# Decoder layer with two experts per row: the outer stage of the mixture folded into its tiles, left-out rounds moved ahead

## The reference

```python
probs = softmax(flat @ gate_W); topk_w, topk_idx = top_k(probs, 2)
topk_w = topk_w / topk_w.sum(-1)
combine = (one_hot(topk_idx, 8) * topk_w[..., None]).sum(1)
out = 0.5 * gelu(flat @ shared_W + shared_b)
for e in range(8):
    h = gelu(flat @ W1[e] + b1[e])                  # 256 -> 1024
    out = out + combine[:, e:e+1] * (h @ W2[e] + b2[e])   # 1024 -> 256
out = layernorm(out) * gamma + beta
x = x + out
```

## Time and profile before

| | |
|---|---|
| median of 3 runs | 792.94 us (788.49, 792.95, 792.94) |
| the profiled execution | 788.47 us, its span 786.6 |
| TensorE busy, matmul | 714.2 us (91%) |
| VectorE, ScalarE, GpSimd busy | 304.1, 443.9, 147.2 us |
| granted TensorE clock, mean | 0.971 of full speed |
| moved by DMA | 126.23 MB, mean 160 GB/s |

### The profile page before, as it was taken

The page is one execution under the profiler, slowest core; times in us unless marked ns, Lnnn a source line. Parts: engine busy times, 40 slices in busy tenths (PEclk is TensorE's granted clock), DMA queues, the critical chain, the costliest instruction groups (busy, mean ns, idle before and its releaser), DMA issues. The chain is left out here.

```text
span 786.6 us, 19149 instructions
## 1 busy us (share of the span) xinstructions
PE 714.2 (91%) x7240; PEld 476.2 (61%) x7241; DVE 304.1 (39%) x1010; ACT 443.9 (56%) x759; POOL 147.2 (19%) x140
## 2 busy tenths in 40 slices
PE   4978999999999999998998989999999999999720
PEld 2435445454544444444454566999999999999710
DVE  5772311201152544549666472145312211221136
ACT  2746989988898988965745541332333233233213
POOL 2020050100000000020012343144222212212414
PEclk9997999999999999999999999999999999999875
DMA  9576948982113030307435346767767677777444
GB/s 206 145 231 190 295 122 280 294 258 65 35 50 103 3 104 15 90 22 238 144 118 162 112 159 232 246 175 212 212 176 208 208 193 205 193 207 205 78 120 107
DMA packets 83858, 126.23 MB, mean 160 GB/s; under 512 B 11090, under 2 KB 69740, under 8 KB 81450
## 3 DMA queue, kind: packets, MB, share of 16 engines
q1 hardware_dynamic: 76248, 114.26, 47.1%
q0 software_dynamic: 7536, 10.95, 7.9%
HBM read 82.85 MB, written 42.33 MB: 159 GB/s over the span
## 5 line engine op out<-in xcount | busy, mean ns | idle before, releaser
L844 ACT ACTIVATE arena<-ps 128x1024 f32<-128x1024 f32 x256 | 240.9, 1034 | 32.9 <-PE ps L1858 32.8
L1858 PE MATMUL ps<-arena 99*32 99x512 bf16 x2048 | 161.9, 388 | 2.8 <-issue 2.4
L1835 PE MATMUL ps<-arena 128*32 128x256 f32 x2048 | 158.5, 380 | 0.0
L2188 PE MATMUL ps<-arena 128*128 128x128 f32 x1120 | 133.6, 279 | 4.9 <-issue 4.0
L2188 PEld LDWEIGHTS ps<-arena 128*128 128x128 f32 x1120 | 132.9, 195 | 7.4 <-issue 4.3
L2200 PE MATMUL ps<-arena,xh_tag 128*128 x560 | 126.8, 379 | 1.2 <-DVE arena L1584 1.2
L2200 PEld LDWEIGHTS ps<-arena,xh_tag 128*128 128x128 f32 x560 | 103.7, 190 | 14.2 <-issue 1.6
L955 ACT COPY arena<-ps 128x256 f32<-128x256 f32 x35 | 13.0, 372 | 163.2 <-PE ps L2175 163.2
L748 POOL DMA_INDIRECT sums_by_row<-arena x39 | 60.2, 1544 | 204.2 <-DVE arena L1584 203.0
L1835 PEld LDWEIGHTS ps<-arena 128*32 128x32 f32 x2048 | 65.1, 111 | 51.9 <-issue 1.9
L966 ACT ACTIVATE xh_tag<-ps,arena 128x128 f32<-128x128 f32 x280 | 76.5, 392 | 10.3 <-PE ps L2188 10.3
(11 more groups left out here) (249 smaller groups left out, 771.0 us busy)
## 6 DMA issues: line engine op xcount, KB each, us to landing
arena<-in_L_ffn_W SPq DMA_DIRECT2D x43, 1024.0 KB, 6.9
rows_by_expert<-arena SPq DMA_DIRECT2D x9, 1950.0 KB, 14.8
arena<-q_parts SPq DMA_DIRECT2D x90, 128.0 KB, 2.6
arena<-k_parts SPq DMA_DIRECT2D x42, 128.0 KB
q_parts<-arena SPq DMA_DIRECT2D x12, 384.0 KB, 2.5
arena<-rows_by_expert SPq DMA_DIRECT2D x35, 130.0 KB, 3.1
arena<-in_L_ffn_b SPq DMA_DIRECT2D x35, 128.0 KB, 3.1
k_parts<-arena SPq DMA_DIRECT2D x8, 384.0 KB, 2.5
```

Source lines behind the costliest of these rows:

```text
L844: nc.scalar.activation(probs_of(stage, h), ps[:, 2 * (u % 2):2 * (u % 2) + 2, :].rearrange("p a n -> p (a n)"), ACT.Exp, scale=float(D) ** ...
L1835: last = nc.tensor.matmul(ps[32 * h:32 * h + 32, 4 + half, at:at + 256], v_grp[n % 2][:, kt, h, :], probs_of(stage, h)[:, 256 * part:256 * ...
L1858: last = nc.tensor.matmul(ps[c:c + 32, 2 * (u % 2) + half, :], k_stk[buf][:, h, P * st + c:P * st + c + 32], q_stk[buf][:, h, 512 * half:5 ...
L2188: last = nc.tensor.matmul(ps[:, 4 * buf + half, P * c:P * (c + 1)], w1_buf[:, buf, k, at:at + P], xs_t[:, buf, k, :], start=(k == 0), stop ...
```

## The change

Each row's tags now say which of its two experts is the higher (`min` of the two ranks, one operation in `choose`), and carry two addresses, one for the lower expert's result and one for the row. `sums_dram` goes; `parts_dram` has 3 x 256 values for each row: the first expert's weighted result, the shared product, and x plus beta. In the tile of the lower expert the weighted result of a row is written to the first part (`write_first`). In the tile of the higher expert all three parts are gathered (`read_parts`), VectorE adds them to its own result, normalises with a root of its own (three Newton steps), applies gamma and adds x (`normalised`), and the row goes to the output (`write_out`). Rows for which a transfer is not meant have an address out of bounds. The last stage is gone, and so is the accumulating transfer.

The rounds that may be left out now come first: `begin` branches by the flags once, to one of four written-out starts, which raise the semaphores by what the left-out slots would have given. GpSimd has no branch: its queue runs through all 39 slots. The tile table is shifted by the left-out slots. The column of b1 is copied by ScalarE, results alternate between two banks (`Y_BANK`), x plus beta is formed by GpSimd ahead of the scatters of chunks 0 to 2 and by VectorE for chunk 3 and stored by SyncE (eight stores; six of them, with the first four of the eight base stores, before the first W1). The rows scattered are 262 values wide, not 260, and 2 MB of `parts_dram` are zeroed where 0.9 MB of `sums_dram` were.

```diff
+        def begin(eng, flags, start):
+            def from_round(k):
+                if k == MAYBE:
+                    start(k)
+                    return
+                with eng.If_ne(flags[MAYBE - 1 - k], 0):
+                    start(k)
+                with eng.If_eq(flags[MAYBE - 1 - k], 0):
+                    from_round(k + 1)
...
+            def start_sp(k):
...
+                sp.wait_ge(scattered, 16 * 2 * NT)
+                for j in range(2):
+                    load_rows(slots_of(2 * k + j), j)
+                    load_b2(expert(2 * k + j), j)
+                sp.wait_ge(x_last, 1)
+                store_part(3, 2, x_sb, x_out)
+                for ch in (2, 3):
+                    store_base(ch)
+                sp.wait_ge(xs_ps, 2 * k + 1)
+                sp.wait_ge(tag_ready, 2 * k + 1)
+                load_rows(slots_of(2 * k + 2), 0)
...
-            for n in range(1, 2 * SURE + 2):
-                if n >= 2:
-                    pool.wait_ge(sums_set, 16 * (n - 1))
-                add_result((n - 1) % 2, n, row_used[:, (n - 1) % 2:(n - 1) % 2 + 1], sums_set)
...
+            pool.wait_ge(parts_zero, 16)
+            pool.wait_ge(base_out, 16 * 2 * (NT // CHUNK))
+            pool.wait_ge(x_out, 16 * 2 * (NT // CHUNK))
...
+            def read_parts(s):
+                pool.wait_ge(tag_ready, s + 1)
+                if s >= 1:
+                    pool.wait_ge(y_landed, 16 * s)
+                if s >= 2:
+                    pool.wait_ge(out_ready, s - 1)
+                nc.gpsimd.indirect_dma_start(out=parts_in[:, s % 2, :], out_offset=None, in_=parts_dram, in_offset=rows_at(last_row_at, s),
+                                             bounds_check=NT * P - 1, oob_is_err=False).then_inc(parts_landed[s % 2], 16)
+            def write_first(s):
+                pool.wait_ge(y_ready, s + 1)
+                nc.gpsimd.indirect_dma_start(out=part_rows, out_offset=rows_at(first_row, s), in_=y_sb[:, s % 2, :], in_offset=None,
+                                             bounds_check=3 * NT * P - 1, oob_is_err=False).then_inc(y_landed, 16)
+            def write_out(s):
+                pool.wait_ge(out_ready, s + 1)
...
+            read_parts(0)
+            for s in range(FINAL):
+                write_first(s)
+                read_parts(s + 1)
+                write_out(s)
+            write_out(FINAL)
...
+            def tags(buf, s):
...
+                nc.vector.scalar_tensor_tensor(out=weight, in0=tag[2], scalar=rank, in1=tag[3], op0=ALU.is_equal, op1=ALU.mult)
+                nc.vector.scalar_tensor_tensor(out=last, in0=tag[5], scalar=rank, in1=skipped, op0=ALU.is_equal, op1=ALU.mult)\
+                    .then_inc(tag_half, 1)
+                dve.wait_ge(tag_half, s + 1)
+                nc.vector.tensor_tensor(weight, weight, tag[4], ALU.add)
+                nc.vector.tensor_tensor(first_row[:, at], tag[0], last, ALU.add)
+                nc.vector.tensor_tensor(last_row_at[:, at], tag[1], last, ALU.subtract).then_inc(tag_ready, 1)
...
+            def normalised(buf, s, landed):
...
+                dve.wait_ge(parts_landed[buf], landed)
+                dve.wait_ge(y_ready, s + 1)
+                linked(nc.vector.tensor_tensor(z_sb, parts_in[:, buf, 0:D], parts_in[:, buf, D:2 * D], ALU.add))
+                linked(nc.vector.tensor_tensor(z_sb, z_sb, y_sb[:, buf, :], ALU.add))
+                nc.vector.memset(ln_t, 0.0)
+                linked(nc.vector.bn_stats(ln_stats, z_sb))
+                nc.vector.memset(ln_t, 0.0)
+                linked(nc.vector.bn_aggr(ln_mv, ln_stats))
+                linked(nc.vector.tensor_scalar(ln_v[0], ln_mv[:, 1:2], 4e-5, None, ALU.add))
+                nc.vector.tensor_scalar(ln_v[1], ln_v[0], 0.25, None, ALU.mult)
+                nc.vector.tensor_scalar(ln_v[2], ln_v[0], 0.0625, None, ALU.mult)
+                linked(nc.vector.tensor_scalar(ln_t.bitcast(I32), ln_v[0].bitcast(I32), 1, None, ALU.logical_shift_right))
+                linked(nc.vector.tensor_scalar(ln_r.bitcast(I32), ln_t.bitcast(I32), -1.0, float(0x5F3759DF), ALU.mult, ALU.add))
+                for v in ln_v:
+                    linked(nc.vector.tensor_scalar(ln_t, ln_r, ln_r, v, ALU.mult, ALU.mult))
+                    linked(nc.vector.scalar_tensor_tensor(out=ln_r, in0=ln_t, scalar=-3.0, in1=ln_r, op0=ALU.add, op1=ALU.mult))
...
+            def round_dve(i):
                 for o in range(2):
...
+                    s = 2 * i + (o + 1)
+                    tags(o, 2 * i + (o + 2))
+                    result(1 - o, s, 16 * i + 16 * (o + 1))
+                    normalised(1 - o, s, 16 * i + 16 * (o + 1))
```

More of the change, by code:

```diff
@@ L348, in decoder_layer, with run_flags @@
         block = scope.enter_context(nc.Block())
[L350 to L364, removed]
+        def run_flags(on):
+            flags = [on.alloc_register(f"run_{i}_{on.engine.name}") for i in range(MAYBE)]
+            for i, flag in enumerate(flags):
+                on.reg_load(flag, run[0:1, i:i + 1])
+            return flags
+        def begin(eng, flags, start):
[7 more added lines that the diff above has]
+                    from_round(k + 1)
+            from_round(0)
         def queries_written(eng, n):
@@ L626, in step @@
                 e = expert(j + 1)
-                sp.wait_ge(y_ready, j)
+                if not (isinstance(j, int) and j == 0):
+                    sp.wait_ge(y_ready, j)
                 load_b2(e, 1 - buf)
             sp.wait_ge(slot_ready, NT // CHUNK + 1)
[L631 to L643, removed]
             def round_sp(i):
@@ L655, in _ @@
-            e = expert(final)
-            sp.wait_ge(y_ready, SLOT_TILES - 2)
-            load_b2(e, 0)
[L658 to L670, removed]
@@ L673, in _ @@
+            begin(sp, run_flags(nc.sync), start_sp)
+            with sp.Fori(MAYBE, PAIRS) as i:
+                round_sp(i)
+            e = expert(FINAL)
+            sp.wait_ge(y_ready, FINAL - 1)
+            load_b2(e, 0)
+            for buf in range(2):
+                sp.wait_ge(out_landed[buf], 16 * (PAIRS + 2 - buf))
         @block.gpsimd
@@ L735, in _ @@
             for ch in range(NT // CHUNK):
+                if ch < 3:
+                    pool.wait_ge(xh_ready, NT + CP + CHUNK * (ch + 1))
+                    for t in range(CHUNK * ch, CHUNK * (ch + 1), 2):
+                        last = nc.gpsimd.tensor_tensor(x_sb[:, t:t + 2, :], x_sb[:, t:t + 2, :],
+                                                       ffn_b_sb.unsqueeze(1).to_broadcast([P, 2, D]), ALU.add)
+                    last.then_inc(x_final, 1)
+                else:
+                    pool.wait_ge(u_ps, 2 * 4)
+                    for rows in (first_row, last_row_at):
+                        last = nc.gpsimd.iota(rows, [[0, SLOT_TILES]], base=int(SKIPPED), channel_multiplier=0)
+                    last.then_inc(indices_set, 1)
+                    pool.wait_ge(indices_set, 1)
+                if ch == 0:
+                    pool.wait_ge(rows_set, 4)
                 pool.wait_ge(slot_ready, ch + 1)
@@ L752, in _ @@
-            for n in range(1, 2 * SURE + 2):
-                if n >= 2:
-                    pool.wait_ge(sums_set, 16 * (n - 1))
-                add_result((n - 1) % 2, n, row_used[:, (n - 1) % 2:(n - 1) % 2 + 1], sums_set)
-                if n <= NT // 2:
-                    rows = x_sb[:, 2 * n - 2:2 * n, :]
-                    last = nc.gpsimd.tensor_tensor(rows, rows, ffn_b_sb.unsqueeze(1).to_broadcast([P, 2, D]), ALU.add)
-                if n == NT // 2:
-                    last.then_inc(x_shifted, 1)
@@ L1545, in _ @@
             link(nc.vector.tensor_scalar(expert_rank, expert_rank, float(EXPERTS), None, ALU.add))
-            for i in range(SURE, PAIRS):
-                last = nc.vector.tensor_scalar(run_f[:, i - SURE:i - SURE + 1], ends[:, EXPERTS - 1:EXPERTS], 2.0 * i + 3, None, ALU.is_gt)
-            link(last)
-            nc.vector.tensor_copy(run, run_f)
-            link(nc.vector.tensor_reduce(last_f, run_f, AX.X, ALU.add))
-            nc.vector.tensor_scalar(last_tile, last_f, 2.0, 2.0 * SURE + 2, ALU.mult, ALU.add)
@@ L1672, in _ @@
+            begin(dve, run_flags(nc.vector), start_dve)
+            with dve.Fori(MAYBE, PAIRS) as i:
+                round_dve(i)
+            tags(0, FINAL)
+            for s in (FINAL - 1, FINAL):
+                result(s % 2, s, 16 * (s // 2 + 1))
+                normalised(s % 2, s, 16 * (s // 2 + 1))
         @block.tensor
```

395 lines of the change are left out of this document (191 added, 204 removed).

## The result

The changed kernel takes **876.96 us** (median of 4, 874.67 to 880.03) beside 792.77 for the kernel before (median of 4): a ratio of 1.107, 95% interval 1.103 to 1.111. The forecast was 798 us with a range of 782 to 816. That was 5 us above the 792.94 of before, next to no change; the kernel is 84 us slower. The profiled span is 874.1 us, 87.5 above the one of before.

A forecast was written before the change was run, and what follows sets the result against it. TensorE was taken to bound the expert stage, with a ragged end and serial last stage. Terms: -24.8 (end) + 24.5 (start) + 5.6 (tiles) = +5.3, a span near 792; scaled to the median, 798 us, range 782 to 816.

The forecast's parts named there:

- What bounds the stage: Steady expert tiles: TensorE's 7.25 us a tile bounds them, and delays queued behind the normalisation lose 5.6 us over 30 tiles.
- 0.75 late ... x = 0.19: Gathered rows reach VectorE 0.75 us late, delaying W1; a ring of three tiles then adds 0.19 us per tile.
- The 2.6 of the scatter: Landing time in us assumed for a plain scatter, in the expert tiles and the last tile's chain.
- The 3.9 of the gather: Landing time in us assumed for a usual tile's gather, the accumulating transfer's median; bounds 3.1 and 5.1.
- Rival 3: Expert tiles: the normalisation becomes the ring that sets the tile, losing 19 us instead of 5.6: 811 us; chance 0.30.
- Rival 4: Indirect transfers with a bounds check cost what the accumulating one does: 10 us more at the start, 808 us; chance 0.08.
- The normalisation on VectorE: Work added per expert tile: 4.6 us, bounds 4.0 and 5.6; VectorE then needs 6.6 of 7.25 us, not the bound.
- The start: Start of the expert stage: empty transfers chained behind the stores delay the first real gather: 21.8 us lost, 24.5 with the clock.
- Rival 2: Start of the expert stage: empty transfers are nearly free, so the turn is only 6 us late: 781 us; chance 0.20.
- The rest at nothing: Moved adds to x cost 0 to 2 us; zero fill, choice, tile table and wider tags under 1 us together.
- The end: After the last steady tile: ragged end and serial last stage shrink, 24.8 us saved; 16.4 us from last matmul to end.
- The ragged end: Final tiles' matmuls: 10.8 us left after the last steady second layer instead of 18.7, so 7.9 us saved.

The follow-up runs named there:

- small_w1: Changed kernel with the loop's loads of W1 cut to an eighth, so values are wrong: 815.64 us, ratio 1.030.
- scatter_apart: Changed kernel with the scatter sent to a DRAM tensor of its own and the gather not waiting for its landing; first expert's result missing: 789.31 us, ratio 0.995.
- lagged: Changed kernel with each tile normalised behind the next tile's result and its output written one step later, nothing left out: 796.91 us, ratio 1.0055.
- start_fixed_no_empty: Changed kernel with the start written in, without flags or branches, and GpSimd's four empty slots left out; right for these inputs alone: 861.16 us, ratio 1.089.
- before_with_adds: Kernel before the change, with only GpSimd's additions of the bias to x for the first three chunks put in: 795.11 us, ratio 1.0044.
- no_adds: Changed kernel without GpSimd's additions to x in chunks 0 to 2, so the output lacks beta there: 873.58 us, ratio 1.102.

## Why the prediction was wrong

**What bounds the stage: the step that failed.** "0.75 late ... x = 0.19" gave +5.6 us; measured +73.3. Two faults stand in it. The first is the price of the landings. The 2.6 of the scatter came from the attention stage, where five loads of 1 MB lay in 73 us. The 3.9 of the gather, bounded above by 5.1, was that of the accumulating transfer: it stood beside the loads of W1 already, but moves 1 KB a row where the gather moves 3. In the two tiles shown the landings were 4.8 and 6.5. The row of W1, 6.7 us out of each 7.25, said that a 1 MB load is in flight nearly all the time, and here the scatter is issued about 1 us behind one (W1 at 660.76, scatter at 661.77). The accumulating transfer was issued 1.9 us ahead of one (606.06 and 607.98); that this order matters is likely, but no run shows it apart. The second fault is larger: the ring was the wrong one. I followed the delay through W1 over three tiles, and never added up the circle of scatter, gather, normalisation, tags and result. At my own prices it is 0.75 + 2.6 + 0.75 + 3.9 + 4.6 + 0.85 + 0.85 = 14.3, so 7.15 a tile against 7.25: no slack to speak of, where each microsecond on a landing costs half a microsecond on every tile. With the two landings put in it is 19.1, so 9.55 a tile; 9.69 was measured. small_w1 shows the first fault (the longest landings fall by 2 to 2.6), scatter_apart and lagged the second. Rival 3 came nearest, at 0.30 ("the normalisation becomes the ring"), but its 811 us used 5.1 for the gather, and left the scatter at 2.6. Rival 4 had the wrong price: an indirect transfer with a bounds check takes 1.0 us to issue, not 1.54, and an empty one can land after 2.1.

**The normalisation on VectorE** was right: 4.81 (654.25 to 659.06) against 4.6. The part missed is the Newton step with two scalars read from SBUF, 0.27 in place of 0.16, three times. The 6.6 us that VectorE needs for a tile is right as well: from one result (660.13) to the next (666.74) are 6.61 us, of which it is busy for about 5.8; it waits for no other engine between them. That left 0.6 us a tile.

**The start** was too small: 35.0 against 21.8 at the fifth turn. The form was right in each link: VectorE waiting for the gather (until 540.72), empty transfers at 1.3 us in front, landings not free. The chain from the end of the stores to the gather's landing took 28.1 us, priced 26.2 (slots of 6.1, 7.9, 5.6, 5.6, priced 5.7). From there to the turn it was 7.7, priced 9.0, since the rows landed sooner. What failed is its first date: 512.6 (513.36 - 0.75), not 500. Of these 12.6 us 10.6 are the last chunk's scatter, which came later (a part of that by the choice of execution, as said), and all stores stand behind it. Sum: 12.6 + 1.9 - 1.3 = 13.2. Rival 2 (empty transfers nearly free) falls: start_fixed_no_empty gives 21.0 at the turn. Of the Trainium skill, "DMA: Bandwidth & Descriptors", "Anatomy of one DMA — SWDGE (gpsimd) path", the fixed cost of about 2.0 us agrees with the shortest landings (2.1 and 2.2).

**"The rest at nothing"** failed. The moved additions cost 3.0 us (before_with_adds) to 3.4 (no_adds), priced 0 to 2. The price forgot what comes behind the held operation: TensorE idle for 2.19 us and a mean clock of 0.79 in the 16 us after it. The row of 2.55 us was read, and put aside. The Trainium skill ("SBUF — State Buffer", "Who interferes with whom") is borne out by 0.16 becoming 3.16 us beside GpSimd's addition. The flags and branches, allowed for with "something", cost SyncE 7.4 us and TensorE 5.5 at the first turn; that matters only once the chain and the ring are gone. The rest of the delay ahead of the stage is open. The first chunk's scatter comes 3.2 us later before any addition to x can matter (412.00 against 408.85, and 409.01 in before_with_adds); the larger zero fill and the wider tags are there, but no run separates them. In the other eight profiles with the changed attention stage that scatter comes at 409.86 to 415.50, so much of the 3.2 may be the spread of executions.

**The end** was right within 4 us: -20.8 against -24.8. From the last matmul (853.77) to the end are 20.4 us, priced 16.4. The result of the tile before the last was ready at 855.27, not at 851.3, since VectorE stood in the normalisation that had waited 4.82 for its gather: the ring again. The ragged end is gone as forecast: two second layers back to back, 7.07 us for 32 at full speed.

## What to carry to other kernels

When a transfer is put between two steps of a loop, add up the whole circle through it, at once and over as many iterations as it spans, and divide: a circle within 2% of the bound is a bound as soon as one landing is longer. Price landings from a stretch in which the same large loads are in flight, and from a transfer of the same size. If the circle is closed by a result that is not wanted at once, take it one iteration later; here two moved calls gave back 80 of 84 us. Count what an unrolled queue issues for work that is left out, and put it where the queue waits anyway.

## What the runs showed of the hardware

An indirect transfer of GpSimd with every index out of bounds is not free: 1.0 us to issue, 1.29 from one to the next, and it lands after 2.1 us at the least (6.7 in one case, behind the stores at the start); when each waits for the one before it, a slot of three costs 5.6 to 7.9 us. Indirect transfers are held up by the hardware queue's loads: the same scatter and gather land after up to 6.3 and 6.7 us beside a 1 MB load, and 4.3 and 4.1 beside one of an eighth.
